# A two-layer transformer on one core: projections, attention and quantized FFN of the first layer, in three stages or in one

## The reference, cut to what matters

```python
# x: (8, 512, 128) float32, two layers
xn = layernorm(x)
x = x + attention0(xn) + quantized_ffn0(xn)
xn = layernorm(x)
x = x + attention1(xn) + moe_ffn1(xn)       # 8 experts, silu(x wg) * (x wu) wd, summed

# attention: 16 heads of 8, causal, softmax, output projection; layer 0 has biases
qkv = xn @ attn_w.T + attn_b
probs = softmax(where(mask, k q / sqrt(8), -10000))
out = (probs v) @ out_w.T + out_b

# quantized FFN: blocks of 32 along the last axis share an exponent, 3 bits of mantissa
h = gelu(block_quant(xn) @ block_quant(w_fc).T + b_fc)      # 128 -> 512
ffn = block_quant(h) @ block_quant(w_proj).T + b_proj        # 512 -> 128
```

## Time and profile before

| | us |
|---|---|
| median of three runs | 1597.89 (1596.04 to 1610.23) |
| the profiled execution | 1593.13, span 1591.4 |
| TensorE busy | 1425.7 (90%), mean granted clock 0.927 |
| VectorE busy | 1135.7 (71%) |
| ScalarE busy | 787.5 (49%) |
| GpSimd busy | 677.3 (43%) |

### The profile page before, as it was taken

The page is one execution under the profiler, slowest core; times in us unless marked ns, Lnnn a source line. Parts: engine busy times, 40 slices in busy tenths (PEclk is TensorE's granted clock), DMA queues, the critical chain, the costliest instruction groups (busy, mean ns, idle before and its releaser), DMA issues. The chain is left out here.

```text
span 1591.4 us, 23490 instructions
## 1 busy us (share of the span) xinstructions
PE 1425.7 (90%) x7944; PEld 818.4 (51%) x7944; DVE 1135.7 (71%) x3279; ACT 787.5 (49%) x1183; POOL 677.3 (43%) x784
## 2 busy tenths in 40 slices
PE   3788699999999956649999999999999999999987
PEld 1444344444444423426666666666666666666655
DVE  4887667767767726748787878777778787887843
ACT  2333245555555522216565656565655656565640
POOL 5555122222222213536455555455654554655540
PEclk9656589999999977869999999999999999999997
DMA  4322423333333212451112121111121211111003
GB/s 126 86 72 75 94 54 83 73 92 76 82 90 77 63 39 81 144 125 43 39 30 59 30 59 30 39 50 39 31 58 36 52 36 39 30 39 39 15 18 111
DMA packets 55333, 97.55 MB, mean 61 GB/s; under 512 B 8999, under 2 KB 19372, under 8 KB 52398
## 3 DMA queue, kind: packets, MB, share of 16 engines
q1 hardware_dynamic: 55214, 96.06, 23.7%
HBM read 51.98 MB, written 41.95 MB: 59 GB/s over the span
## 5 line engine op out<-in xcount | busy, mean ns | idle before, releaser
L206 POOL TENSOR_SCALAR_AFFINE_SELECT a_E<-a_E 128x256 f32<-128x256 f32 (+1 forms) x384 | 188.1, 493 | 555.0 <-ACT a_E L985 311.8
L1185 POOL TENSOR_TENSOR a_h_lo<-a_h,a_h_hi 128x512 fp32r<-128x512 f32 x256 | 329.3, 1286 | 150.2 <-ACT a_h_hi L1232 143.3
L182 DVE CUSTOM_DVE_ANT_0 bank<-bank,mask 128x512 f32<-128x512 f32 (+3 forms) x512 | 242.1, 516 | 117.6 <-PE bank L143 117.4
L1293 DVE SCALAR_TENSOR_TENSOR a_h<-a_h,bank 128x512 f32<-128x512 f32 x256 | 175.6, 686 | 150.9 <-ACT a_h L1228 150.9
L985 ACT ACTIVATE a_E<-bank_pair 128x1024 f32<-128x1024 f32 (+1 forms) x192 | 169.1, 881 | 173.4 <-PE bank_pair L153 173.2
L182 DVE CUSTOM_DVE_ANT_0 bank_pair<-bank_pair,mask 128x512 f32<-128x512 f32 (+3 forms) x512 | 238.0, 516 | 8.3 <-PE bank_pair L143 8.0
L1239 ACT ACTIVATE a_E<-bank_pair 128x1024 f32<-128x1024 f32 (+1 forms) x192 | 169.7, 884 | 134.3 <-PE bank_pair L153 134.1
L1369 PE MATMUL bank<-xT_hi,a_w_hi 128*128 128x512 f32 x512 | 215.3, 421 | 6.6 <-DVE a_h L1293 6.6
L1232 ACT ACTIVATE a_h_hi<-a_h 128x512 fp32r<-128x512 f32 x256 | 160.8, 628 | 118.3 <-DVE a_h L1299 116.6
L1371 PE MATMUL bank<-xT_lo,a_w_hi 128*128 128x512 f32 x512 | 203.7, 398 | 0.0
L1370 PE MATMUL bank<-xT_hi,a_w_lo 128*128 128x512 f32 x512 | 203.1, 397 | 0.0
(11 more groups left out here) (124 smaller groups left out, 1877.0 us busy)
## 6 DMA issues: line engine op xcount, KB each, us to landing
a_st<-stack_d SPq DMA_DIRECT2D x128, 160.0 KB
a_st<-stack_d SPq DMA_DIRECT2D x256, 64.0 KB
o_d<-a_O SPq DMA_DIRECT2D x64, 256.0 KB, 2.3
stack_d<-p_q_k_hi SPq DMA_DIRECT2D x48, 256.0 KB
stack_d<-p_q_k_lo SPq DMA_DIRECT2D x32, 256.0 KB
stack_d<-p_max_rows SPq DMA_DIRECT2D x2, 1024.0 KB, 9.3
a_st<-a_ms SPq DMA_DIRECT2D x128, 16.0 KB
at<-o_d SPq DMA_DIRECT2D x8, 256.0 KB, 3.6
```

The source lines that it names most:

```text
L182: ins = nc.vector.tensor_tensor_reduce(part, part, mask[:, N - w:N], 1.0, NEG, ALU.add, ALU.max, mx[:, g % 2, NT - 1 - kb, PLANES * r + j: ...
L206: return nc.gpsimd.affine_select(out=part, in_=part, compare_op=ALU.is_ge, fill=0.0, base=0, pattern=pattern, channel_multiplier=-1)
L1185: nc.gpsimd.tensor_tensor(h_lo[:, q % RH, :], h[:, q % RH, :], h_hi[:, q % RH, :].bitcast(F32), ALU.subtract).then_inc(h_lo_ready, 1)
L1293: nc.vector.scalar_tensor_tensor(hq, hq, 1.0, g_bank[:, :], ALU.add, ALU.mult).then_inc(silu_ready, 1)
```

## The change

`project(0)`, `attend` and `project(1)` become one block, `layer0`, of 46 steps, -7 to 38. Step g carries quad g of the attention: S of quad g+1, T of g-1 (units 3 to 5) and g (units 0 to 2), PV of g-1. With b = g // 4 and u = g % 4, it also carries one FFN tile (g+3) of the first layer, and by u a part of the first layer's projections of batch b+1 or b+2, of the attention output of batch b-1, and of the second layer's projections of batch b-2.

S now uses 32 rows and one pair of banks: the two halves r of a unit go into the two banks, and two more matmuls (`identb` by the mask, bf16, 128 columns) add the mask to the last block. VectorE takes plain maxima over both banks at once, six a quad. T has one pair of banks in place of two, and `keep_warm` is gone. The maxima bank is the first bank of the S pair. The Gelu is one operation over two banks. The biases of queries and keys are added by ScalarE. The fixed rows of the image are set once in SBUF in place of a 2 MB image in DRAM. The reciprocals of the denominators are spread through DRAM (`rden_d`, `share`), the product with them is GpSimd's. `E` has three slots in place of four. `attend_moe` gets the three images from outside, and loads 16 rows in place of 20 for each half in its first load.

```diff
+        T_pair, S_pair, W_pair, pv_bank, C_bank = *pairs, banks[6], banks[7]
+        A_bank, B_bank, M_bank = W_pair[:, 0, :], W_pair[:, 1, :], S_pair[:, 0, :]
+        QT = C_bank[:, 0:N // 2].bitcast(BF16)
...
+            for step in range(-7, QUADS + 7):
+                yield step, step // QUADS_A_BATCH, step % QUADS_A_BATCH
...
-def keep_warm(nc, pair, identb, mask):
-    for r in range(HALVES):
-        nc.tensor.matmul(pair[:, r, :], identb[:, :], mask[:, :], start=True, stop=True)
...
+            def maxima_of(g, n):
+                dve.wait_ge(S_ready, UNITS_A_QUAD * g + n + 1)
...
+                if n < 4:
+                    t, j = NT - 1 - n % 2, n // 2
+                    out = mx[:, g % 2, t, :].rearrange("p (r j) -> p r j", j=PLANES)[:, :, j]
+                    src = S_pair[:, :, 0:P * (t + 1)]
+                else:
+                    t = 5 - n
+                    out = mx[:, g % 2, t, :]
+                    src = S_pair[:, :, :].rearrange("p r (j c) -> p (r j) c", j=PLANES)[:, :, 0:P * (t + 1)]
+                nc.vector.tensor_reduce(out, src, AX.X, ALU.max).then_inc(S_used, 1)
...
+            def S(g, n):
+                if n == 0:
...
+                    if g > 0:
+                        pe.wait_ge(mrow_ready, g)
+                else:
+                    pe.wait_ge(S_used, UNITS_A_QUAD * g + n)
+                t = NT - 1 - n % 2 if n < 4 else 5 - n
+                w = P * (t + 1)
+                for j in ((n // 2,) if n < 4 else range(PLANES)):
+                    at_col = j * N // PLANES if n >= 4 else 0
+                    for r in range(HALVES):
+                        rows = slice(HALF * r, HALF * r + SLOT_ROWS)
+                        nc.tensor.matmul(S_pair[:, r, at_col:at_col + w], st[g % STACKS][rows, j, 0, bass.ts(t, P)],
+                                         st[g % STACKS][rows, j, 1, 0:w], start=True, stop=False)
+                    for r in range(HALVES):
+                        ins = nc.tensor.matmul(S_pair[:, r, at_col + w - P:at_col + w], identb[:, :], mask[:, N - P:N], start=False, stop=True)
+                ins.then_inc(S_ready, 1)
...
             def T(g, n):
                 if n == 0:
                     pe.wait_ge(mrow_in, MAX_LOADS * (g + 1))
-                if UNITS_A_QUAD * g + n >= 2:
-                    pe.wait_ge(exp_done, UNITS_A_QUAD * g + n - 1)
-                keep_warm(nc, T_pair(g, n), identb, mask)
-                keys_by_queries(nc, T_pair(g, n), st, g % STACKS, n % 3, n // 3).then_inc(T_ready, 1)
+                if g > 0 or n > 0:
+                    pe.wait_ge(exp_done, UNITS_A_QUAD * g + n)
+                keys_by_queries(nc, T_pair, st[g % STACKS], n % 3, n // 3).then_inc(T_ready, 1)
```

More of the change, by code:

```diff
@@ L225, in build @@
         xT = sb("xT_hi", [P, B * N], F32R), sb("xT_lo", [P, B * N], F32R)
[L226 to L234, removed]
+        stacks = [sb(f"st{i}", [P, PLANES, 2, N], F32R) for i in range(MOE_STACKS)]
@@ L370, in _ @@
-            for b in range(B):
-                store(b, b % 2)
-            for p in range(2):
-                sp.wait_ge(parts_out[p], START + STORES * B // 2)
-        def schedule(eng, before, batch, after):
-            before()
-            for b in range(B):
-                batch(b, b + 1 if b + 1 < B else None, b + 2 if b + 2 < B else None, b % 2, b // 2)
-            after()
+                    sp.wait_ge(ready, 2 * m + i + 1)
+                    for slot in IMAGE_SLOTS[part][i]:
+                        row = slot * HD * PLANES
+                        sp.dma_start(halves[:, row:row + HD * PLANES, i, :], parts[:, m % 2, i, :].bitcast(F32)).then_inc(parts_out[m % 2], 16)
@@ L665, in _ @@
-            DVE_STEPS = 2 * NT + 2 * (1 + NT) if first else 2 * NT
-            def after():
-                if first:
-                    unshift_tile(B - 1, NT - 1)
-                    add_ffn(B - 1)
-            schedule(dve, before, batch, after)
+                    here.inc(nc.vector.bn_aggr(mv[layer][:, t, :], stats[layer][:, t, :]))
+                here.ready()
+                nc.vector.tensor_scalar(veps[layer][:, :], mv[layer][:, :, 1], LN_EPS, None, ALU.add).then_inc(var_ready[layer], 1)
@@ new lines, in queries, with keys, values @@
+            def queries(layer, b):
+                pe.wait_ge(xnT_ready[layer], b + 1)
+                nc.tensor.matmul(A_bank[:, :], wq[layer][:, :], xnT[layer][:, :], start=True, stop=True).then_inc(qk_ready, 1)
+            def keys(layer, b):
+                if layer == 1:
+                    pe.wait_ge(xhi_ready, b + 1)
+                nc.tensor.matmul(B_bank[:, :], wk[layer][:, :], xnT[layer][:, :], start=True, stop=True).then_inc(qk_ready, 1)
+            def values(layer, b, bank):
+                for t in range(NT):
+                    ins = nc.tensor.matmul(bank[:, bass.ts(t, D)], xnT[layer][:, bass.ts(t, P)], wv[layer][:, :], start=True, stop=True)
+                ins.then_inc(vals_ready[layer], 1)
@@ L1107, in _ @@
[L1107 to L1113 removed]
+                    maxima_rows(g + 1)
+                if u == 0 and ok(b + 1):
+                    fc(b + 1, 1)
+                if g == FIRST + 1:
+                    pe.wait_ge(w_in, 16 * SMALL_LOADS)
+                    turn_weight(0)
+                    turn_weight(1)
@@ L1116, in attend_moe @@
+def attend_moe(nc, xT, acc, experts, pairs, banks, consts, st, st_d, o_d):
     wg_in, wu_in, wd_in = experts
```

1307 lines of the change are left out of this document (616 added, 691 removed).

## The result

The changed kernel took **1813.1 us** (median of 4 runs, 1807.9 to 1826.7) against 1600.3 for the kernel before on the same chip: a ratio of 1.133 (95% interval 1.125 to 1.142). Forecast were 1715 and a range to 1785: the sign was right, the size was not. The profiled execution has a span of 1807.0 us and a time of 1808.7.

The account below looks back on a forecast made before the run. First and third stages were taken as chains of waits, `attend` as TensorE busy 382 of 408 us. New stage 60 + 32 x 22.3 - 16 + 47 = 805 against 688, 117 slower: 1593 + 117 + 5 = 1715 us, range 1540 to 1785.

Parts of the forecast that it names:

- 30% of the time at the upper level: `layer0`: TensorE gets the upper clock 30% of the time, one or two rises in four steps; mean step 22.3 us.
- mostly low with rises: `layer0`: clock at the upper level 10 to 50%, mean step 20.6 to 24.3 us, total 1658 to 1779; chance 0.50.
- the missing guests: `layer0`: steps without some of their added projection or FFN work save 16 us in the stage.
- rival 2: `layer0`: the clock stays low, no dense part dense long enough; step 25.4, stage 904, total 1814 us; chance 0.10.
- keeps its code but for 16 rows loaded in place of 20, so I give it no change: Mixture stage with the second attention, 872 us, TensorE busy for 840: no change in time.
- last step and tail: End of `layer0`: after step 31, T and PV, then an uncovered serial chain for the last batch, 47 us.
- P at the upper clock, 17.35: `layer0`: mean of the 32 steps carrying a quad, at 2.4 GHz, 17.35 us, bounds 15.9 to 19.
- At the lower clock: `layer0`: mean of the 32 steps carrying a quad, at 1.2 GHz, 25.4 us, TensorE's queue nearly the chain.
- rival 3: `layer0`: projections hide little in in-order queues; keys, values and queries uncovered add 2 us a step, +64 us.
- The table loads: `layer0`, ScalarE: two loads in four steps, between Gelu and exp, 2.6 us on the path.
- rival 4: `layer0`: ScalarE's table reloads for Gelu and exp dominate; four loads in four steps instead of two, +20 us.
- rival 1: `layer0`: the clock holds, no thin stretch lowers it; step 17.35, stage 639, total 1549 us; chance 0.26.

Follow-up runs that it names:

- the run on 36 rows: The changed kernel with the mixture stage's scores on 36 rows in place of 32: 1791.8 us.
- With fills: Changed kernel plus 512-column matmuls at six places (two each, four behind the `fc` step) and at step ends, mixture-stage scores on 36 rows: 1629.8 us.
- the thin projections: The 1629.8 us version with f32 projection matmuls cut to an eighth or a quarter, for all batches but the first: median 1648.4 us.

## Why the prediction was wrong

**The step that failed: "30% of the time at the upper level"**, and the case it stands for, "mostly low with rises". It was 12%. The formula itself is nearly right: 1/(0.12/17.35 + 0.88/25.4) = 24.1, less 0.5 for the missing guests 23.6, and 24.0 was measured. I had counted on one or two rises in four steps from the dense parts. The step has the dense parts, and the clock comes up only in a few pieces (0.55 and 0.52 in the second and third step of the batch shown). Where it comes up and goes down is as I had said: in the profile after it rises in the PV group at 621.7 us and has fallen by the scores at 637.6 (256 columns take 0.38 us in a T pair at 634.5 and 0.58 in a pair of scores at 637.6), among scores and T. What was wrong is how often a dense part is enough. The rows of 200 to 212 us of the kernel before misled me: there `keep_warm` was at work too, and PV seemed to be what brought the clock up. Without `keep_warm` scores, T and PV stay at 0.50 for 360 us. Of the 94 us between forecast and profiled execution, 31 periods of 24.0 instead of 21.8 (the forecast mean, with the missing guests in it) make 69.

**A coincidence.** The measured 1813 lies beside the 1814 of rival 2, "the clock stays low". This is luck: its stage of 904 us is 30 too long (873.6 was measured, at 12% of the upper level and not none), and the mixture stage, to which it gives nothing, makes up for just these 30.

**The second: "keeps its code but for 16 rows loaded in place of 20, so I give it no change".** +30 us, of which the run on 36 rows takes back 23. The rest of the sum: step 0 starts at 65.4, not 60 (+5), and last step and tail take 63.1, not 69 (-6). 69.3 + 30.1 + 5.4 - 5.7 = 99.1, less the 4.8 that I had added for the median and that the profiled time doesn't have: the 94, but for rounding.

The Trainium skill has a rule that fits this ("TensorEngine Tiling (Array Packing)", Tiling Modes): a change of the array's tiling mode, not of the tile alone, drains TensorE. It lists a mode with tiles of 32 rows, which hold 32 rows but not 36. The trace agrees with a price of each change, 0.09 us (0.43 against 0.34) and 0.05 again behind T; that it is this drain no run here shows.

**P at the upper clock, 17.35.** With fills a full batch gave 19.05. What the fills cost can be read where only their number differs: step 3 took 16.7 us with six of them in a step and 17.4 with twelve, step 30 16.1 and 16.8, so 0.7 for six. The batch of 19.05 has twelve in three of its steps and 24 in one, a mean of fifteen, 1.75 by this price: my estimate for a step without fills is 17.3 (17.7 if the extra twelve cost nothing), beside the forecast and inside its bounds. It assumes that the first six cost what the second six do, and leaves in what the fills at the end of a step cost. **At the lower clock** the batch shown gives 26.1 at 0.52, against 25.4.

**The parts.** Reductions, masks (two together 0.39 at the lower level, 0.28 at the upper, for 0.25), and the hidden projections came out as forecast or near it; rival 3 is refuted by the thin projections. The table loads are there, two a batch, but only 0.5 of the 2.6 us that I had put on the path, so of rival 4 nothing is left at the upper clock.

**The rule that I had weighed.** The Trainium skill's rule on idle gaps ("TensorE: Matmul & The Clock Gate", HAM oscillation — how this bites in real kernels) gave rival 1, to which I gave 0.26. The rows against it: 0.50 for 360 us with TensorE busy for 96% of them, and a fall behind an idle piece of no more than 1.02 us. Gaps alone don't explain it; the one of 2.02 us was closed and the clock was lost in the thin part all the same.

**Rival 1's time** was too low as well: with the clock at 1.00 for most of the stage the kernel takes 1630, not 1549. Stage by stage the profiled execution (1631.6) is 87 us longer than what that rival adds up to without its 4.8 for the median: 7 at the start, 66 in the 31 periods, 5 in the last step and tail, 9 in the mixture stage. Of the 66 the fills make 43 to 54 by the estimate above; the rest stays open. The first stage takes 717 us with the clock held, against 688 in the kernel before, so by this estimate the price of holding the clock eats what the merge gains. No version made here is faster than the kernel before; the best one is 1.4% (0.9 to 1.9) behind it.

## What to carry to other kernels

Before work is merged to fill an engine's waits, ask what the filler that is removed was doing for the clock: a TensorE busy for 96% of the time with matmuls of few rows can be granted half its clock, and a stage that then waits for it pays for every merged matmul at that clock (two 512-column f32 matmuls 2.02 us in place of 1.08). If fills are needed, put them ahead of waits, into a bank that is idle, in the thinnest stretch and in the full dose; half of it cost more than none (1812 against 1790, both with fills at the end of the step). And look at the number of rows of neighbouring matmuls before changing one of them: saving four rows of 36 cost 0.7 us in 26.

## What I hadn't expected of the hardware

- At the six places, twelve fills a step hold the clock in three steps of four, six hold it in hardly any and give 1812, and 24 in the thinnest step with twelve in the others hold it in all from the eighth on (these three with fills at the end of the step as well).
- The clock stayed at 0.50 through 360 us in which TensorE was idle for 13 us in all, on scores and T of 36 rows, PV of 9 columns and the transposes of the maxima.
- From 32 to 36 rows and back: 0.14 us for a pair of scores and T.
- A higher clock can be worth nothing: 0.70 in place of 0.56 for 1817 in place of 1813, where the matmuls that raise it stand behind the wait for the exp.
